# A pairwise-interaction tower: 49 quads a chunk, a pacing mark for every gather, deeper one-hot slots

## The reference, cut to what matters

```python
e = jnp.stack([tbl_0[ids[:, 0]], ..., tbl_39[ids[:, 39]]], axis=1)   # 2048 x 40 x 32
vi = e[:, I, :]; vj = e[:, J, :]                                      # the 780 pairs i < j
z = jnp.einsum('bke,kef,bkf->bk', vi, W, vj)                          # W: 780 x 32 x 32
h = jnp.concatenate([z, dense_ctx], axis=1)                           # 2048 x 796
h = jnp.maximum(h @ W_top1 + b_top1, 0.0)                             # 512 wide
h = jnp.maximum(h @ W_top2 + b_top2, 0.0)                             # 256 wide
y = h @ W_top3                                                        # 2048 x 1
```

## Time and profile before

| | us |
|---|---|
| median of 3 runs | 658.86 (657.85 to 658.96) |
| the profiled execution: its span | 861.5 |
| PE busy | 747.6 |
| DVE busy | 540.2 |
| POOL busy | 402.1 |
| ACT busy | 241.3 |

### The profile page before, as it was taken

How to read it: one execution, slowest core, us unless ns; L and a number is a source line. 1 busy time by engine, 2 the same in 40 slices (tenths; PEclk the granted TensorE clock), 3 DMA queues, 4 the chain that set the end, 5 groups by cost and what they waited for, 6 DMA issues and landing times.

```text
span 861.5 us, 11435 instructions
## 1 busy us (share of the span) xinstructions
PE 747.6 (87%) x4928; PEld 222.9 (26%) x4928; DVE 540.2 (63%) x513; ACT 241.3 (28%) x181; POOL 402.1 (47%) x423
## 2 busy tenths in 40 slices
PE   4768886898889799998899999799988979998998
PEld 1212221222222122222222222222222222222333
DVE  6666665686557566574656658665656665775840
ACT  3524643756123234434302233400000000000002
POOL 6735463454526356446445645454645645453000
PEclk9979997998979889899998889999999989998999
DMA  8712202011201202010111010100110110100100
GB/s 264 254 32 70 70 11 60 17 34 46 72 26 29 69 8 63 18 32 12 46 46 47 11 45 11 45 11 8 48 45 11 48 45 11 46 11 7 37 1 1
DMA packets 26963, 38.08 MB, mean 44 GB/s; under 512 B 9552, under 2 KB 16352, under 8 KB 26784
## 3 DMA queue, kind: packets, MB, share of 16 engines
q1 hardware_dynamic: 13568, 30.49, 10.8%
q0 software_dynamic: 13312, 6.84, 5.3%
q10 hardware_dynamic: 32, 0.01, 0.0%
HBM read 22.36 MB, written 0.01 MB: 26 GB/s over the span
## 4 chain that ended last, share of the span: by engine, by line
PE 63%; another core or an unknown queue 16%; DVE 9%; ACT 7%; issue 3%; DMA 1%; DVEq 0%; SPq 0%; ACTq 0%
PE tps L729 24%; PE zps L751 17%; PE mlp_ps L802 12%; DVE prods L707 8%; PE mlp_ps L782 7%; PE tps L802 3%; ACT hot L561 3%; ACT hot L564 3%; DMA zs<-in_hot_table 1%; ACT zs L530 0%; ACT parts L553 0%; PE zps L738 0%; ACT eT L579 0%; DVE hot L650 0%
## 5 line engine op out<-in xcount | busy, mean ns | idle before, releaser
L707 DVE TENSOR_TENSOR prods<-tps,eT 128x1024 f32<-128x1024 f32 x400 | 469.6, 1218 | 264.6 <-PE tps L729 141.4
L514 POOL DMA_INDIRECT rows<-in_table,idx x416 | 401.5, 965 | 381.7 <-DVE prods L707 257.4
L729 PE MATMUL tps<-eT,weights 32*128 32x512 f32 x1600 | 302.0, 677 | 62.8 <-DVE prods L707 42.3
L751 PE MATMUL zps<-prods,select 128*32 128x512 f32 x1600 | 224.7, 652 | 13.5 <-ACT zs L530 10.6
L729 PEld LDWEIGHTS tps<-eT,weights 32*128 32x128 f32 x1600 | 87.1, 194 | 231.2 <-DVE prods L707 113.7
L782 PE MATMUL mlp_ps<-hot,parts 128*32 128x512 bf16 x1344 | 113.3, 421 | 27.8 <-issue 10.8
L561 ACT ACTIVATE hot<-ids,minus_code 128x2048 bf16<-128x2048 int16 x47 | 93.8, 1995 | 67.3 <-PE mlp_ps L782 46.6
L802 PE MATMUL mlp_ps<-zs,w1s 128*128 128x512 f32 x182 | 94.3, 649 | 6.8 <-ACT eT L579 6.8
L564 ACT ACTIVATE hot<-hot,ones 128x2048 bf16<-128x2048 bf16 x47 | 94.1, 2002 | 1.5
L751 PEld LDWEIGHTS zps<-prods,select 128*32 128x32 f32 x1600 | 38.7, 112 | 178.4 <-issue 112.0
L530 ACT ACTIVATE zs<-zps 128x512 f32<-128x512 f32 x28 | 16.7, 597 | 211.5 <-PE zps L751 123.3
(11 more groups left out here) (29 smaller groups left out, 50.1 us busy)
## 6 DMA issues: line engine op xcount, KB each, us to landing
eT<-eT SPq DMA_DIRECT2D x38, 192.0 KB
ids<-in_hot_ids SPq DMA_DIRECT2D x14, 512.0 KB
rows<-in_table,idx POOLq DMA_INDIRECT x416
eT<-eT SPq DMA_DIRECT2D x38, 128.0 KB
eT<-eT SPq DMA_DIRECT2D x38, 64.0 KB
zs<-in_hot_table SPq DMA_DIRECT2D x4, 512.0 KB, 7.9
w1s<-in_w SPq DMA_DIRECT2D x1, 1792.0 KB
weights<-in_wt SPq DMA_DIRECT2D x1, 960.0 KB
```

Source lines behind the costliest of these rows:

```text
L514: pool.indirect_dma_start(rows[:, k % ROW_SLOTS, m * EMB:(m + 1) * EMB], None, table, bass.IndirectOffsetOnAxis(ap=idx[:, g, t, m:m + 1], ...
L707: dve.tensor_tensor(prods[:, at % PROD_SLOTS, 2 * half:2 * half + 2, :], tps[:, (2 * at + half) % PAIR_BANKS, :, :], tiles, ALU.mult).then ...
L729: last = pe.matmul(tps[:, (2 * at + half) % PAIR_BANKS, bank, :], weights[part, n, :], eT[part, slot_of(t, g), :], start=True, stop=True)
L751: last = pe.matmul(zps[EMB * r:EMB * (r + 1), :], select[:, off:off + EMB], prods[:, at % PROD_SLOTS, bank, :], start=kt < KT - 1 and slot ...
```

## The change

- **49 quads a chunk** (196 in place of 200). For pairs of groups after the first, `pair_quads` and the table `WINS` choose six mixed tiles of four fields instead of three; `SP` makes them with 13 or 14 copies (`runs_of`, `COPIES`) in place of 6. Two quads of a pair now stand four quads behind the first use of its second group; those of the pair (2, 3) are put behind three quads of the next pair.
- **Aligned twos**: every chunk begins with a cycle of one quad, and all others are twos. Before, only the first and the last cycle of all had one quad.
- **Steps** are cut 3, 2, 2 (and 2, 2 in the second layer) in the second and third chunk; before 4, 3 or 7 or 4 in the second and 2, 2, 3 in the third.
- **Hot groups** 4, 4, 4, 3: one more group is looked up, 16 gathers fewer (400).
- **Look-ups** of two units behind one quad (four a cycle) in the second and third chunk, before one unit; 7 slots of `hot` instead of 4.
- **Makers**: ScalarE makes 24 of the 32 units of the second chunk (before 21), VectorE 8.
- **A mark at every gather** (`PARTS_AT`), due times from the same planner.
- Room is found by a 4 KB ring for GpSimd's descriptors (`dynamic_dma_scratch_size`, 16 KB by default), 12 slots of `zs` for 14, and indices for seven groups only.

```diff
+def pair_quads(p):
+    c, g = 2 * p, 2 * p + 1
+    if p == 0:
...
+    blocks = [(mover % Q, c + mover // Q, ("mix", p, WIN_TILES[p].index(fields)) if mover < 2 * Q - 1 else ("group", c))
+              for mover, fields in WINS[p].items()]
+    loser = next(mover for mover in range(Q) if mover not in WINS[p])
+    return [[blocks[-1]] + blocks[Q - 1:-1], [(loser, 3, ("group", 0))] + blocks[:Q - 1]]
...
-        quads += of_c + of_g[:2] + both + of_g[2:]
+        of_g = [[(r, g, ("group", other)) for r in range(Q)] for other in range(c) if (g, other) != (3, 0)]
+        early = 1 if p == 1 else Q
+        quads += of_c[:Q - 1] + (pair_quads(1) if p == 2 else []) + of_c[Q - 1:] + of_g[:early]
+        quads += (pair_quads(p) if p != 1 else []) + of_g[early:]
...
-HOT_COUNT = (4, 4, 4, 2)
+HOT_COUNT = (4, 4, 4, 3)
...
-HOT_SLOTS = 4
+HOT_SLOTS, FIRST_UNITS = 7, 4
...
-            starts = list(range(0, len(tile) - 1, 2)) if t > 1 else [0, 4] if at < 2 else [0]
+            starts = [0] + list(range(len(tile) % 2 + 2, len(tile) - 1, 2))
...
-CYCLES = [(0,)] + [(at, at + 1) for at in range(1, TOTAL - 1, 2)] + [(TOTAL - 1,)]
+CYCLES = []
+for t in range(CHUNKS):
+    CYCLES += [(t * QUADS,)] + [(t * QUADS + n, t * QUADS + n + 1) for n in range(1, QUADS, 2)]
...
-                blocks += [(hots[batch[-1][3]], u) for u in range(0, UNITS, 2)]
+                blocks += [(hots[batch[-1][3]], u) for u in range(0, UNITS, FIRST_UNITS)]
...
-    return [g > 1 and u == 5, ((h - HOT_COUNT[0]) * UNITS + u) % 3 > 0, u % 2 == 1][min(t, 2)]
+    return [g > 1 and u == 5, u % 4 > 0, u % 2 == 0][min(t, 2)]
...
-MADE_AHEAD = 4
+MADE_AHEAD = (8, 5, 7, 4, 6, 3, 5, 1)
...
-PARTS_AT = [0, 6, 11]
+PARTS_AT = list(range(GATHERS))
...
+                for k, fields in enumerate(WIN_TILES[p] if p > 0 else []):
+                    for slot, field, count in runs_of(fields):
+                        row = EMB * (field % Q)
+                        sp.dma_start(eT[EMB * slot:EMB * (slot + count), ET_SLOTS + k, :],
+                                     eT[row:row + EMB * count, slot_of(t, 2 * p + field // Q), :]).then_inc(mixed, 16)
```

More of the change, by code:

```diff
@@ L32, with runs_of @@
 MIXES = ((0, 1, 1, 1), (0, 0, 0, 1), (1, 1, 0, 0))
+WINS = {1: {0: (1, 2, 3, 4), 2: (1, 3, 4, 5), 3: (1, 4, 5, 6), 4: (1, 5, 6, 7), 5: (0, 1, 6, 7), 6: (0, 1, 2, 7), 7: (0, 1, 2, 3)},
[3 rows of a table added]
+WIN_TILES = {p: [fields for mover, fields in wins.items() if mover < 2 * Q - 1] for p, wins in WINS.items()}
+MIX_SLOTS = 2 * Q - 2
+def runs_of(fields):
+    runs = []
+    for slot, field in enumerate(fields):
+        if runs and field == runs[-1][1] + runs[-1][2] and field % Q:
+            runs[-1][2] += 1
+        else:
+            runs.append([slot, field, 1])
+    return runs
+def pair_quads(p):
+    c, g = 2 * p, 2 * p + 1
+    if p == 0:
+        mix = [("mix", p, k) for k in range(len(MIXES))]
+        return [[(0, g, ("group", c)), (1, g, mix[2]), (2, c, mix[1]), (3, c, mix[1])],
+                [(0, c, ("group", g)), (1, c, mix[0]), (3, g, ("group", g)), (2, g, mix[2])]]
+    blocks = [(mover % Q, c + mover // Q, ("mix", p, WIN_TILES[p].index(fields)) if mover < 2 * Q - 1 else ("group", c))
+              for mover, fields in WINS[p].items()]
+    loser = next(mover for mover in range(Q) if mover not in WINS[p])
+    return [[blocks[-1]] + blocks[Q - 1:-1], [(loser, 3, ("group", 0))] + blocks[:Q - 1]]
 def plan_quads():
@@ L40, in plan_quads @@
         c, g = 2 * p, 2 * p + 1
-        mix = [("mix", p, k) for k in range(len(MIXES))]
-        both = [[(0, g, ("group", c)), (1, g, mix[2]), (2, c, mix[1]), (3, c, mix[1])],
-                [(0, c, ("group", g)), (1, c, mix[0]), (3, g, ("group", g)), (2, g, mix[2])]]
         of_c = [[(r, c, ("group", other)) for r in range(Q)] for other in range(c)]
-        of_g = [[(r, g, ("group", other)) for r in range(Q)] for other in range(c)]
-        quads += of_c + of_g[:2] + both + of_g[2:]
+        of_g = [[(r, g, ("group", other)) for r in range(Q)] for other in range(c) if (g, other) != (3, 0)]
+        early = 1 if p == 1 else Q
+        quads += of_c[:Q - 1] + (pair_quads(1) if p == 2 else []) + of_c[Q - 1:] + of_g[:early]
+        quads += (pair_quads(p) if p != 1 else []) + of_g[early:]
     return quads
@@ L84, in last_quad @@
     return [n for n in range(QUADS) if g in groups_of(n)][-1]
+COPIES = [2 * len(MIXES)] + [sum(len(runs_of(fields)) for fields in WIN_TILES[p]) for p in range(1, GROUPS // 2)]
 MIXED = [[n for n in range(QUADS) if mixed_of(n) == p] for p in range(GROUPS // 2)]
@@ L153, in plan_sides @@
         for u in range(UNITS):
[L154 removed]
+            sides[at + u // FIRST_UNITS].append(("hot", h, u))
     own = HOT_COUNT[0]
@@ L162, in plan_sides @@
         hots = [h for h, (t_, _) in enumerate(HOTS) if t_ == t + 1]
-        twos = range(t * QUADS + 1, (t + 1) * QUADS, 2)
+        twos = [cycle[0] for cycle in CYCLES if t * QUADS <= cycle[0] < (t + 1) * QUADS]
         blocks = []
@@ L174, in plan_sides @@
                 h, u = block
-                sides[at].append(("hot", h, u))
-                sides[at + 1].append(("hot", h, u + 1))
+                for unit in range(u, u + FIRST_UNITS):
+                    sides[at + (unit - u) // 2].append(("hot", h, unit))
             else:
@@ L215, in by_scalar @@
     t, g = HOTS[h]
-    return [g > 1 and u == 5, ((h - HOT_COUNT[0]) * UNITS + u) % 3 > 0, u % 2 == 1][min(t, 2)]
+    return [g > 1 and u == 5, u % 4 > 0, u % 2 == 0][min(t, 2)]
 def made_until(h, u, scalar):
     return sum(by_scalar(h_, u_) == scalar for h_ in range(len(HOTS)) for u_ in range(UNITS) if (h_, u_) <= (h, u))
-MADE_AHEAD = 4
+MADE_AHEAD = (8, 5, 7, 4, 6, 3, 5, 1)
 MAKES = {at: [] for at in range(TOTAL)}
-MAKES[0] = [(2, u) for u in range(HOT_SLOTS, UNITS)]
+MAKES[0] = [(2, u) for u in range(FIRST_UNITS, UNITS)]
 for unit in range(UNITS):
-    MAKES[3 if by_scalar(3, unit) else 1 + unit // HOT_SLOTS].append((3, unit))
+    MAKES[3 if by_scalar(3, unit) else 1 + unit // FIRST_UNITS].append((3, unit))
 for side_at, items in SIDES.items():
@@ L459, in mix @@
                 wait(sp, multiplied, 2 * (t_ * QUADS + MIXED[p_][-1] + 1))
-                for k, sides in enumerate(MIXES):
+                for k, sides in enumerate(MIXES if p == 0 else []):
                     for side in range(2):
@@ L681, in _ @@
             rest(2, 0)
-            for u in range(HOT_SLOTS):
+            for u in range(FIRST_UNITS):
                 make_unit(2, u)
```

37 lines of the change are left out of this document (21 added, 16 removed), and 3 rows, old and new, of the table WINS.

## The result

The changed kernel took 660.78 us (median of 9 runs, 659.13 to 661.10), the kernel before beside it 658.18 us (9 runs, 656.95 to 660.05): a ratio of 1.0032 with a 95% interval of 1.002 to 1.0044. Forecast was 656.0. So the change makes this kernel slower by a third of a per cent, where a gain of 0.4% was expected; the time lies inside the range given, on its upper side.

The account below looks back on a forecast made before the run. TensorE's instruction list was taken as the bound. Its priced cycles gave -1.2 us and the end -1.7, other terms 0: -2.9 from 658.86, so 656.0 us, with a range of 651 to 662.5.

Parts of the forecast that it names:

- Makers ... I take 0: ScalarE's and VectorE's one-hot units: ScalarE 88% loaded in the first chunk (before 78%), cost 0, range -1 to +4 us.
- One-unit cycles: TensorE cycles with one look-up unit (16 matmuls), 5.01 us each: 10 before at 50.1, 12 after at 60.1.
- ScalarE late in the first chunk: Rival, chance 0.08: three units in a row outlast four quads; TensorE waits 1 to 2 us, three times; 660 us.
- The single cycles: Three chunks begin with one quad and 3, 3 and 2 steps: 4.77 us twice and 3.91, together 13.5.
- Four and seven steps: TensorE cycles with batches of 4 or 7 steps, 7.92 and 10.4 us; cutting them was to save 1.6 us.
- two-step cycles: TensorE cycles with two steps, 5.91 us each: 31 before at 183.2, 42 after at 248.2.
- the start: Time ahead of TensorE's first transform, put at 27.5 us instead of the profiled 32.52.
- no gain: Rival, chance 0.12: 48 matmuls behind two quads starve VectorE (+4 us), single cycles cost half a us more; 659 us.
- The end: From the last full reduce to the last MLP: 2.9 us instead of 4.58, so -1.7 us, up to 1.0 possibly lost.
- gathers late: Rival, chance 0.15: GpSimd's gathers late for the transpose of the first chunk's group 7; 2 to 5 us once, 660.
- hidden waits go: Rival, chance 0.12: waits within the 10.5 us above the priced sum vanish, ten mixes at 0.4 us: -4, 652 us.
- The copies: SP's 14 copies per mix: 13 x 0.6 + 2.8 = 10.6 us of 13.1 available in the first chunk, so cost 0.

Follow-up runs that it names:

- the kernels with 21 and 16: The changed kernel with ScalarE making 21 or 16 instead of 24 of the second chunk's 32 one-hot units: 655.91 us (0.9947) and 656.98 us (0.9965).
- the undisturbed trace: Stand-in for the kernel before: that kernel with one mark per gather instead of one for each of three parts, span 655.9 us, ratio 0.9986.
- act21_c: The changed kernel with ScalarE making 21 instead of 24 of the second chunk's 32 one-hot units: 655.91 us against 658.87, ratio 0.9947.

## Why the prediction was wrong

The forecast was a difference of -2.9 us; the traces show +1.4 (655.9 to 657.3), the medians +2.6. The traced execution of the changed kernel was its fastest, 1.6 us under its median. By the table, the 4.3 us between -2.9 and +1.4 come from these steps:

- **"Makers ... I take 0": the failed step.** One-unit cycles were priced 9.3 us too low after and 4.4 too low before; the difference of 4.9 is the one cycle at quad 41. The sum beside it was nearly right: 96 us of units and 5.4 of drains in 115, 88%. The mistake is what was made of it. The margin was averaged over the chunk, and "four units run in a row at most between drains, as before" looked at the longest pack, not at the time that TensorE leaves for each. (It was wrong as well: five stand in a row ahead of the sum drained at 103.77, four before.) Four and five did no harm, since ScalarE still idled 5.5 and 1.3 us ahead of their drains (81.73 and 103.77); three did, where the drain of a group and the drain of a sum lie 10.0 us apart for TensorE and 12.3 for ScalarE. With two units there (8.35 us) the wait is gone. The rival "ScalarE late in the first chunk" is what happened, at the time it named (660), with a chance of 0.08, and its first clause ("three units in a row take 12 us where four quads last 10.4") is the mechanism. Its condition, a lead used up, is not: ScalarE had just idled. Its price was shaped otherwise: not 1 to 2 us three times, but once, 2.94 us and 1.7 more at the lower clock. That the units cause it is shown by the kernels with 21 and 16; that it is the three in a row at this place, rather than their number in the chunk, is read from the traces, since no run kept the 24 and moved one away.
- **The single cycles: 3.4 us.** Priced 4.77, 4.77 and 3.91, measured 5.97, 5.83 and 5.09. The prediction took a transform and a reduce off a cycle, and forgot that the eight `place` matmuls of the dense inputs stand in these three; they take 1.06 us in the row of L783 above. Before, they were in cycles of two quads, where they added 0.45 us each in the undisturbed trace (6.36 instead of 5.91, twice, and 8.10 instead of 7.63). That costs the change some 2 us, 0.7 at each of three chunk boundaries. Not tried apart; it is read from the two timelines.
- **Four and seven steps: 1.0 us.** They were priced at 52.5 and took 51.5 before, so cutting them saved 1.0 less than the -1.6 claimed. The prices of adding steps were the right ones; the earlier trace rows had been drawn out by the disturbance.
- Other terms took 5.0 us back: empty cycles 1.2, two-unit cycles 1.7, two-step cycles 1.8 (three of them at 5.37 to 5.44, light ones at a chunk's end; and two of before at 6.36, those with `place` matmuls), the start 0.6, less 0.3 for four and eight units. The start varies by 1.7 us between executions (25.4 to 27.1 in seven undisturbed traces), so its part says nothing on the change.

What held. The prices read from undisturbed cycles of a bad trace: 5.91, 6.77, 5.37 to the hundredth, and 6.72 fourteen times for the 48 matmuls that were put at 6.69 by addition, with no starving of VectorE ("no gain"). The end: 33.2 against a forecast of 33.3, with a wait of 0.72 for the drain and 2.70 us from the last full reduce's end (624.21) to the last MLP, where 2.9 were given. The rivals "gathers late" and "hidden waits go": no transpose waits (the 64th gather ends at 90.8 us, where 93.6 was given), and the sum's distance to the undisturbed span, part of what had been taken for waits, was three under-priced common terms (one-unit cycles at 5.45 instead of 5.01, eight units at 11.7 instead of 9.2, four at 7.9 instead of 6.7), less 1.5 at the start. The first 32 gathers are slow here too, 1119 ns on average against 970 for all; those that overlap a one-hot of VectorE take 1071, the others 946, which fits what the prediction made of them. In the eight-unit cycle TensorE waits once for VectorE's one-hot (0.7 us) and once for ScalarE's drain (0.7) in both kernels, which can't be added up from matmuls. The copies: SP's own queue in the changed kernel,

```profile
140.56 10.00 SPq L508 DMA_DIRECT2D eT<-eT  x14
```

takes 10.00 us, where 13 x 0.6 = 7.8 to the last issue were given, yet products wait for copies twice only, 0.8 us in all:

```profile
L752 DVE TENSOR_TENSOR prods<-tps,eT 128x1024 f32<-128x1024 f32 x392 | 459.6, 1218 | 91.0 <-PE tps L774 86.9 <-ACT eT L617 1.3 <-DMA eT<-eT 0.8
```

(VectorE's group of products from 30 us on). The margin of 13.1 us was larger than the surprise. The 2.0 us of the Trainium skill (DMA: Bandwidth & Descriptors, Anatomy of one DMA) are given there for DMAs that GpSimd issues, and these are SP's; the trace shows 14 issued 0.7 us apart, so no such cost is paid one after the other here.

The clock's share in the late cycle, 1.7 of 4.6 us, is told by the rows above: a transform of eight takes 2.09 us behind the stop and 1.14 at the upper level. The Trainium skill (TensorE: Matmul & The Clock Gate, What's actually happening) says that the lower clock is the default and activity lifts it; the trace agrees for this stop, at 0.83 granted in its window. A wait like this one so has to be priced above its length; two shorter ones in the same trace, 0.89 us at 147.45 and 0.69 at 47.60, are followed by transforms of 1.14.

Would the change have been a gain had ScalarE kept its share? By act21_c, yes: 0.9947, 655.91 us, next to the forecast of 656.0. The forecast's -2.9 was nearly the right size for that kernel (-3.0), but from terms that partly cancelled, as the table shows.

## What to carry to other kernels

An engine's load averaged over a stage says little when that engine also carries short work that others wait for. Go through its list in order: between two such pieces of work that each wait for another engine, add up what stands there, and compare it with the time that the other engine takes between the same two points. Idle time ahead of the first doesn't help the second. And before an order is called tested, write out the list before and after the edit, since two shifts can cancel. When a list is cut differently, move every instruction of the cut cycle in the sum, also the few that stand there once a chunk. And when a profiled execution is a third longer than the median, its cycles can be priced one by one, but its idle times can't be used.

## What was not expected of the hardware

The same program takes 658 us on some chips and 835 to 855 us on others, with TensorE standing at recurring places of its list for 1 to 7 us, with no release that the profile shows, and slower matmuls after it (mean clock 0.94 instead of 1.00). It depends on the program: the changed kernel takes 747 to 763 us there, with half as many stops, and putting the three marks back for its gathers takes it to 820. A change that can't be told from nothing on one chip (marks in the kernel before, 0.9986 and 0.9994) thus belongs to something that is worth 8% on another, in the changed kernel; what the marks alone do to the kernel before there wasn't measured. What TensorE waits for in these stops stays open.

Second, 14 copies between partitions on one queue take 10.00 us to issue, 0.7 each, where six had taken 0.6 each.
